# Two side buffers and 32 rows a step for ScalarE's pieces in both gather stages of a graph network kernel

## What is computed

```
h = relu(layernorm(x))
# layer 1: each edge fetches the row of its source node, transformed by its edge type
xW  = einsum('nd,rde->nre', h, W_rel)                 # 8 types
agg = segment_sum(xW[src, edge_type], dst)
y   = h + gelu(layernorm(agg + h @ W_self + b_conv) * g1 + b1n)
x   = x + y + gelu((layernorm(y) * g2 + b2n) @ W1 + b1) @ W2 + b2
# layer 2: attention over the same edges, 4 heads
h   = relu(layernorm(x));  xt = h @ W.T + bias
alpha = leaky_relu(alpha_src[src] + alpha_dst[dst])   # softmax over the edges of a target node
out = x + segment_sum(xt[src] * softmax(alpha), dst)
```

## Time and profile before

| quantity | value |
|---|---|
| median of three runs | 4349.86 us |
| time of the profiled execution | 4343.06 us |
| its span in the trace | 4341.3 us |
| POOL busy | 3081.9 us (71%) |
| DVE busy | 2539.8 us (59%) |
| PE busy | 2488.5 us (57%) |
| ACT busy | 860.6 us (20%) |
| mean granted TensorE clock | 0.745 of full speed |

### The profile page before, as it was taken

The page is one execution under the profiler, slowest core; times in us unless marked ns, Lnnn a source line. Parts: engine busy times, 40 slices in busy tenths (PEclk is TensorE's granted clock), DMA queues, the critical chain, the costliest instruction groups (busy, mean ns, idle before and its releaser), DMA issues.

```text
span 4341.3 us, 72570 instructions
## 1 busy us (share of the span) xinstructions
PE 2488.5 (57%) x13901; PEld 2078.1 (48%) x13902; DVE 2539.8 (59%) x7085; ACT 860.6 (20%) x2948; POOL 3081.9 (71%) x3262
## 2 busy tenths in 40 slices
PE   8833444444444444444455676766677667667675
PEld 3333344433433434343344565655566556556564
DVE  7742334444434443444445777777777777777776
ACT  5400111101110111110112222222222222222222
POOL 2177777777777777777737777777777777777774
PEclk9956767767767677677666877778877787787777
DMA  9622222222222222222214222222222222222221
GB/s 322 258 54 55 62 63 59 65 60 62 63 60 64 60 62 63 60 65 61 61 41 115 56 59 62 59 59 62 60 62 60 59 62 60 62 60 60 62 59 44
DMA packets 192089, 314.95 MB, mean 73 GB/s; under 512 B 69617, under 2 KB 123233, under 8 KB 190948
## 3 DMA queue, kind: packets, MB, share of 16 engines
q0 software_dynamic: 103424, 215.33, 21.4%
q1 hardware_dynamic: 38907, 68.15, 4.6%
q10 hardware_dynamic: 49310, 26.90, 2.2%
HBM read 238.52 MB, written 71.59 MB: 71 GB/s over the span
## 4 chain that ended last, share of the span: by engine, by line
POOL 37%; issue 25%; PE 22%; DVE 9%; ACTq 3%; ACT 2%; DMA 1%; DVEq 0%; POOLq 0%; SPq 0%
POOL G L646 37%; PE bank L1773 9%; PE quad L1818 3%; ACTq L819 2%; PE quad L1824 2%; PE quad L1813 1%; DVE A L1302 1%; PE quad L1860 1%; DMA xt_table<-w_all 1%; PE quad L1715 1%; PE bank L1715 1%; PE bank L1716 1%; PE quad L1716 1%; ACT w_all L894 1%; DVE stats L198 1%
## 5 line engine op out<-in xcount | busy, mean ns | idle before, releaser
L646 POOL DMA_INDIRECT G<-rel_table,idx x1600 | 1517.8, 949 | 633.9 <-issue 487.5
L646 POOL DMA_INDIRECT G<-xt_table,idx x1616 | 1526.8, 945 | 545.1 <-issue 545.1
L1906 PEld LDWEIGHTS quad<-ident,top 128*128 128x128 f32 x3328 | 569.4, 269 | 199.1 <-issue 198.2
L1906 PE MATMUL quad<-ident,top 128*128 128x128 f32 x3328 | 582.1, 356 | 119.9 <-DVEq L1507 119.7
L1267 DVE SCALAR_TENSOR_TENSOR agg<-bank,sel,agg 128x128 f32 x208 | 63.7, 347 | 821.1 <-PE bank L1773 809.0
L1937 PE MATMUL bank<-M,onehot 128*128 128x132 f32 x3328 | 445.4, 290 | 167.5 <-DVE M L1556 163.1
L1937 PEld LDWEIGHTS bank<-M,onehot 128*128 128x128 f32 x3328 | 411.2, 199 | 199.3 <-issue 199.3
L1773 PE MATMUL bank<-G,M 128*128 128x128 f32 x1616 | 267.3, 343 | 292.4 <-issue 278.6
L1773 PEld LDWEIGHTS bank<-G,M 128*128 128x128 f32 x1616 | 263.5, 259 | 296.7 <-issue 296.7
L1922 PE MATMUL bank<-Z,w_all 128*128 128x8 f32 x832 | 160.2, 321 | 378.4 <-DVEq L1524 253.5
L957 ACT ACTIVATE M<-G,M 128x32 f32<-128x32 f32 x1664 | 363.9, 308 | 13.3
(11 more groups left out here) (324 smaller groups left out, 3521.3 us busy)
## 6 DMA issues: line engine op xcount, KB each, us to landing
side<-rel_table SPq DMA_DIRECT2D x4736, 0.5 KB
side<-xt_table SPq DMA_DIRECT2D x4736, 0.5 KB
rel_table<-G SPq DMA_DIRECT2D x98, 512.0 KB, 3.4
G<-rel_table,idx POOLq DMA_INDIRECT x1616, 2.6
G<-xt_table,idx POOLq DMA_INDIRECT x1616, 7.1
side<-rel_table ACTq DMA_DIRECT2D x1408, 0.5 KB
side<-xt_table ACTq DMA_DIRECT2D x1408, 0.5 KB
xt_table<-w_all ACTq DMA_DIRECT2D x23, 264.0 KB
```

Source lines behind the costliest of these rows:

```text
L646: g.indirect_dma_start(out=G[:, s, c, 0:width], out_offset=None, in_=table, in_offset=bass.IndirectOffsetOnAxis(ap=idx[:, s, c:c + 1], axi ...
L1906: ins = t.matmul(banks[j][:, hd * P:(hd + 1) * P], top[:, j, hd:hd + 1].to_broadcast([P, P]), ident[:, :], start=False, stop=(hd == HEADS ...
```

## The change

ScalarE takes one piece in each of two groups in eight, in both stages: targets 16, 20, 24, ..., 96 (21 in place of 11). They alternate between two side buffers (`side` grows from 4 to 5 pieces, `x_res` shrinks to make room), so a target waits for the one two before it. In the first stage nothing else changes: 32 rows a step, in steps t-2 to t+1. In the attention stage a target takes four steps of 32 rows, t-6 to t-3, in place of eight steps of 16, t-10 to t-3. A step of 32 is two rounds of a load of 16 places and 16 DMAs (`ACT_ROWS = 16`).

```diff
-ACT_STEP = 8
+ACT_STEP = (4, 4)
+ACT_SIDES = 2
+ACT_LEAD, ACT_EACH = (2, 6), (32, 32)
...
-def by_act(g):
-    return ACT_FIRST <= g <= ACT_LAST and g % ACT_STEP == 0
+def by_act(k, g):
+    return ACT_FIRST <= g <= ACT_LAST and g % ACT_STEP[k] == 0
...
-        x_res = sb("x_res", [P, BLOCKS + SPARE, D])
+        x_res = sb("x_res", [P, BLOCKS + 2, D])
...
-        side = sb("side", [P, SIDES + 1, XT])
+        side = sb("side", [P, SIDES + ACT_SIDES, XT])
...
             def act_rows(k, gr, lo, hi):
-                q = ACTED.index(gr)
+                q = ACTED[k].index(gr)
+                b = q % ACT_SIDES
                 if lo == 0:
-                    act.wait_ge(act_line, 16 * (k * len(ACTED) + q + 1))
-                    if k == 0 and q:
-                        act.wait_ge(agg_done, ACTED[q - 1] + 1)
-                    elif k and q:
-                        act.wait_ge(side_moved, MOVED.index(ACTED[q - 1]) + 1)
+                    act.wait_ge(act_line, 16 * (k * len(ACTED[0]) + q + 1))
+                    if k == 0 and q >= ACT_SIDES:
+                        act.wait_ge(agg_done, ACTED[0][q - ACT_SIDES] + 1)
+                    elif k and q >= ACT_SIDES:
+                        act.wait_ge(side_moved, MOVED.index(ACTED[1][q - ACT_SIDES]) + 1)
                     elif k:
-                        act.wait_ge(agg_done, ACTED[-1] + 1)
+                        act.wait_ge(agg_done, ACTED[0][-1] + 1)
                     act_stop(act)
                 for p in range(lo, hi, ACT_ROWS):
                     places = load_places(mybir.EngineType.Activation, k, line[0:1, 2, p:p + ACT_ROWS], ACT_ROWS)
                     for j in range(ACT_ROWS):
-                        act.dma_start(row_into(k, SIDES, p + j), row_at(k, places[j])).then_inc(acted[k], 16)
+                        act.dma_start(row_into(k, SIDES + b, p + j), row_at(k, places[j])).then_inc(acted[k][b], 16)
-            def first_rows(gr):
-                for target in ACTED:
-                    if gr == target - 3:
-                        act_line_load(0, target)
-                    if 0 <= gr - (target - 2) < 4:
-                        act_rows(0, target, (gr - target + 2) * 32, (gr - target + 3) * 32)
-            def att_rows(gr):
-                for target in ACTED:
-                    if gr == target - 11:
-                        act_line_load(1, target)
-                    if 0 <= gr - (target - 10) < 8:
-                        act_rows(1, target, (gr - target + 10) * 16, (gr - target + 11) * 16)
+            def beside_rows(k, gr):
+                each = ACT_EACH[k]
+                for target in ACTED[k]:
+                    n = gr - (target - ACT_LEAD[k])
+                    if 0 <= n < P // each:
+                        act_rows(k, target, n * each, (n + 1) * each)
+                    if n == -1:
+                        act_line_load(k, target)
...
-                    att_rows(gr)
+                    beside_rows(1, gr)
```

More of the change, by code:

```diff
@@ L87, in by_sync, with by_rows, pieces, fetched @@
     return g <= ROW_LAST and g % ROW_OF in ROW_AT
-def by_act(g):
-    return ACT_FIRST <= g <= ACT_LAST and g % ACT_STEP == 0
-def by_rows(g):
-    return by_sync(g) or by_act(g)
+def by_act(k, g):
+    return ACT_FIRST <= g <= ACT_LAST and g % ACT_STEP[k] == 0
+def by_rows(k, g):
+    return by_sync(g) or by_act(k, g)
 ROWED = [g for g in range(GROUPS) if by_sync(g)]
[L100 to L105, removed]
+ACTED = [[g for g in range(GROUPS) if by_act(k, g)] for k in range(2)]
+MOVED = [g for g in range(GROUPS) if by_rows(1, g)]
+def pieces(k, g):
+    return CHUNKS - 1 if by_rows(k, g) else CHUNKS
 def seat2(g):
     return g % SLOTS
-def fetched(place, g):
-    return sum(16 * pieces(k) for k in range(g + 1) if place(k) == place(g))
+def fetched(k, g):
+    place = (seat, seat2)[k]
+    return sum(16 * pieces(k, b) for b in range(g + 1) if place(b) == place(g))
 def side_of(m):
@@ L405, in build @@
         rowed = [[sem(f"rowed{k}_{i}") for i in range(SIDES)] for k in range(2)]
-        acted = [sem("acted0"), sem("acted1")]
+        acted = [[sem(f"acted{k}_{i}") for i in range(ACT_SIDES)] for k in range(2)]
         act_line = sem("act_line")
@@ L464, in rows_there @@
         def rows_there(k, gr):
-            if by_act(gr):
-                return SIDES, (acted[k], 16 * P * (ACTED.index(gr) + 1))
+            if by_act(k, gr):
+                q = ACTED[k].index(gr)
+                return SIDES + q % ACT_SIDES, (acted[k][q % ACT_SIDES], 16 * P * (q // ACT_SIDES + 1))
             b, there = side_of(ROWED.index(gr))
@@ L655, in first_gather @@
                 pool_stop(pool)
-                gather(rel_table, seat(gr), D, gathered[0][seat(gr)], pieces(gr))
+                gather(rel_table, seat(gr), D, gathered[0][seat(gr)], pieces(0, gr))
             for gr in range(SLOTS):
@@ L695, in att_gather @@
                 pool_stop(pool)
-                gather(xt_table, s, XT, gathered[1][s], pieces(gr))
+                gather(xt_table, s, XT, gathered[1][s], pieces(1, gr))
             for s in range(SLOTS):
@@ L844, in load_indices @@
             def load_indices(gr):
-                act.wait_ge(gathered[0][seat(gr)], fetched(seat, gr) - 16 * pieces(gr))
+                act.wait_ge(gathered[0][seat(gr)], fetched(0, gr) - 16 * pieces(0, gr))
                 a.copy(idx[:, seat(gr), :], idx_all[:, gr, :]).then_inc(idx_ready[0], 1)
@@ L902, in quad_scalar @@
                     load_indices(n * SLOTS + FRONT + SLOTS)
-                    first_rows(n * SLOTS + FRONT + SLOTS)
+                    beside_rows(0, n * SLOTS + FRONT + SLOTS)
                 if own:
@@ L912, in quad_scalar @@
                     load_indices(n * SLOTS + FRONT + SLOTS + 1)
-                    first_rows(n * SLOTS + FRONT + SLOTS + 1)
+                    beside_rows(0, n * SLOTS + FRONT + SLOTS + 1)
                 first_gelu(n)
@@ L916, in quad_scalar @@
                     load_indices(n * SLOTS + FRONT + SLOTS + 2)
-                    first_rows(n * SLOTS + FRONT + SLOTS + 2)
+                    beside_rows(0, n * SLOTS + FRONT + SLOTS + 2)
                 forward(n)
@@ L920, in quad_scalar @@
                     load_indices(n * SLOTS + FRONT + SLOTS + 3)
-                    first_rows(n * SLOTS + FRONT + SLOTS + 3)
+                    beside_rows(0, n * SLOTS + FRONT + SLOTS + 3)
                 if own and not last:
@@ L982, in move_side @@
             def move_side(gr):
-                if gr < MAIN and by_rows(gr):
+                if gr < MAIN and by_rows(1, gr):
                     b, there = rows_there(1, gr)
@@ L995, in _ @@
             move_side(2)
-            next_indices(1, 0, 0, fetched(seat2, 0))
+            next_indices(1, 0, 0, fetched(1, 0))
             for i in range(0, (MAIN - 3) // SLOTS):
@@ L1001, in _ @@
                     move_side(gr + 2)
-                    next_indices(1, gr, (s + 1) % SLOTS, fetched(seat2, gr))
-                    att_rows(gr)
+                    next_indices(1, gr, (s + 1) % SLOTS, fetched(1, gr))
+                    beside_rows(1, gr)
                     if s == 1 and i >= LAG:
@@ L1626, in landed_in @@
             def landed_in(gr):
-                there = [(gathered[1][gr % SLOTS], fetched(seat2, gr))]
-                return there + [(side_moved, MOVED.index(gr) + 1)] if by_rows(gr) else there
+                there = [(gathered[1][gr % SLOTS], fetched(1, gr))]
+                return there + [(side_moved, MOVED.index(gr) + 1)] if by_rows(1, gr) else there
             scores(groups, c, 0, 0, landed_in(0))
@@ L1785, in add_group @@
             def add_group(g):
-                landed = [(gathered[0][seat(g)], fetched(seat, g))]
+                landed = [(gathered[0][seat(g)], fetched(0, g))]
                 if g == MAIN - 1:
                     landed = [(last_gathered[k], 16 * CHUNKS // PARTS) for k in range(PARTS)]
-                add_edges(g, seat(g), g % 2, landed, beside=g if by_rows(g) else None)
+                add_edges(g, seat(g), g % 2, landed, beside=g if by_rows(0, g) else None)
             for g in range(2):
```

## The result

The changed kernel takes 4501.77 us (median of 4 runs, 4500.29 to 4504.12) against 4349.52 us for the kernel before (4 runs, 4347.3 to 4353.6). The ratio is 1.0349, with a 95% interval of 1.0337 to 1.0361: slower by 3.5%. Its profiled execution has a span of 4502.1 us, against 4341.3 us.

The account below looks back on a forecast made before the run. POOL's gathers bound both stages; ACT's ring was to bound 84 attention rounds. 4343.06 + 165.3 (84 rounds) - 13.9 (last nine) - 12.5 (first stage) = 4482.0 us, given as 4485 us, range 4435 to 4545.

Parts of the forecast that it names:

- The 3 us added on top: Whole kernel: 4485 us given between 4482 and 4489, as the median of runs was 6.8 us above the profiled execution.
- The bound and the ring: Attention rounds 10 to 93: ACT's rows hold `hit` in an ACT, PE, DVE ring, making ACT the bound, +165.3 us.
- The two signs named ahead: Attention stage: PE's L1922 released by ACT's `hit` in nearly all 84 rounds; POOL at about 360 gathers in 500 us.
- The size of the ring: Attention rounds with rows: L951 to `hit` 15.65 us plus 5.70 us back to L951, 21.35 us a round.
- The 12.37 us for a step of 32: Median for 32 rows in the first stage, applied to attention; second sixteen cost 12.37 - 5.45 = 6.9 us.
- The last nine rounds: Attention rounds after 93, without rows: DVE at its own pace, seven rounds in 123 us instead of 137, -13.9 us.
- The first stage: First gather stage: POOL stays the bound and loses ten gathers of 1.25 us, -12.5 us.
- The other cover: First-stage dense block: PE's 7.11 us wait at the third group absorbs self products delayed some 14 us.
- Rows hidden in ACT's idle time: Rival, attention stage: second sixteen rows fit ACT's idle time, POOL bounds both stages, 4318 us; chance 0.05.
- The cheaper ring: Rival, attention stage: second sixteen rows cost 5.4 us, ring 19.85 us, about 4360 us; chance 0.07.
- the 8.75 taken for sixteen: Attention rounds: L951 to L943 with sixteen rows taken as 8.75 us, before 6.9 us for the second sixteen.
- The first stage lost nothing: Rival, first stage: four filled steps overrun dense blocks, 3 us for each of 21, about 4558 us; chance 0.10.

Follow-up runs that it names:

- the kernel with hit first: Changed kernel with attention rows issued behind the next round's `hit` copy: 4326.14 us, 0.9947 of the kernel before; on another chip 4318.67 us, 0.9950.
- The split kernel: Changed kernel with 16 of each attention step's 32 rows ahead of `hit` and 16 behind: 4319.98 us, 0.9951 of the kernel before.
- the kernel with one load: Changed kernel with one load of 32 places per step instead of two of 16: 4449.44 us, 1.0236 of the kernel before.

## Why the prediction was right

The forecast of 4485 us was 17 us below the measured 4501.77, and the time lies in the range. A little of that closeness is luck. The sum of 4482.0 us was made for a profiled execution, and that of the changed kernel took 4504.12 us, 22 us more. The 3 us added on top stood for runs that take longer than the profiled one, as in the kernel before; those of the changed kernel took less.

**The bound and the ring: right.** The reading of the earlier trace rows that ACT's rows hold `hit`, and of the earlier trace rows that `hit` closes a ring of 5.70 us, held in 84 rounds of 84; that the order in ACT's stream is the cause is shown by the kernel with hit first, which has the same rows and none of the loss. The two signs named ahead came: PE released by ACT's `hit` in 84 rounds, and POOL at 358 gathers in 500 us (about 360 forecast).

**The size of the ring: a little low.** Forecast 15.65 + 5.70 = 21.35 us, measured 15.79 + 5.74 = 21.53 us. The mis-sized terms are small ones: L949 to `hit` 0.14 us, the rest of the ring 0.04. Over 84 rounds they make the 15.6 us between +165.3 and +180.9, the largest part of the 22. The 12.37 us for a step of 32, read in the first stage, carried over: it is the median of the 84 steps of the attention stage too.

**The last nine rounds: right in kind, -10.5 in place of -13.9.** DVE ran at its own pace, but that is slower than the prediction took it: the seven rounds took 126.5 us and not 123. Four in a row take 17.7, 17.5, 18.7 and, with `finish`, 19.5 us. The 17.45 us of the earlier trace rows is the shortest kind, and I had counted all but the rounds with `finish` as 17.3.

**The first stage: right in direction.** All four kinds of step filled fit beside each other; rows of the fourth kind still end 2.8 us before ACT's second copy of the turned block, in the timeline of ACT of the changed kernel:

```profile
1069.60 12.42 ACTq L823 DMA_DIRECT2D side<-rel_table  x32
...
1084.85 0.60 ACT L878 ACTIVATE Y<-quad 128x512 f32<-128x512 f32 x1 [15.85 <-PE quad L1811]
```

The other cover was less sure than the prediction said: it calls the 7.11 us before PE's third group a wait for the gather, but the row says "issue", so it doesn't show what PE waited for.

The gain was 9.5 us in the trace and not 12.5. The two profiles differ in more than the change: the median gather takes 947 ns in the one of the changed kernel and 944 ns in the one before, and 3 ns over 1590 gathers are some 4 us. The split kernel and the second profile of the one with hit first have the same first stage and gathers of 944 ns; there L951 of round 10 starts at 2528.8 and 2526.7 us, 11.4 and 13.5 us before the 2540.2 of the earlier trace rows. So the 12.5 us are borne out.

**The rivals.** Rows hidden in ACT's idle time (4318 us) failed for the place, not for the amount: with the rows behind `hit`, they are hidden, and the gain is near the 25 us worked out for that rival (24, and 22 on another chip). The cheaper ring was refuted: with 32 rows ahead L949 to `hit` is 15.79 us, 7 more than the 8.75 taken for sixteen, and not 5.4. The first stage lost nothing.

**What issuing costs.** The Trainium skill says in "DMA: Bandwidth & Descriptors", section "Issuing engines are not separate DMA queues", that initiating a DMA is "usually small relative to the DMA itself". The prediction was right not to take the rows as free, but its words that this trace disagrees go too far for a single row. The last landing of a step came some 3 us after its last row was issued (by the semaphore updates in the trace of the changed kernel), while a step without a load in its middle holds ACT's stream for 10.74 us, or 0.34 us a row. What counts here is that the issues of 32 rows stand one behind another: in the round shown, 29 of them with a load of places held the stream for 10.89 us. What the same section says of several issuing engines, that they only save the sequencer's time, agrees with the kernel with hit first: it gained 24 us, where twenty gathers of 1.25 us left POOL.

## What to carry to other kernels

Issuing a DMA isn't counted as busy, but it holds the instruction stream of its engine: 32 row DMAs with the load of addresses in their middle took 12 to 13 us. Before such work is given to an idle-looking engine, find the ring of waits that passes through it, read its length from the one round in which this engine was the last, and put the work behind the step that others wait for. Here, against the kernel before, the same instructions made +152 us ahead of one copy and -24 us behind it.

## What the runs showed of the hardware

- The load of places (TENSOR_LOAD) on ACT took 1.19 us for 16 values and 2.14 us for 32. The second load of a step, right behind sixteen row DMAs, took 1.31 us on average in the changed kernel. So one load of 32 saves only 0.24 to 0.36 us against two of 16.
- A gather on POOL isn't of quite constant length. Its median is the same in both stages of one profile, and differs between profiles: 944, 945 or 947 ns. The line of the gathers of the first stage, of the changed kernel and of the second profile with hit first, which have the same first stage:

```profile
L650 POOL DMA_INDIRECT G<-rel_table,idx x1590: 941/947/2323, 203.1 to 2199.4; - x199
...
L650 POOL DMA_INDIRECT G<-rel_table,idx x1590: 940/944/2323, 203.1 to 2197.0; - x199
```

  The mean from start to start goes with it: in the first stage 1.254 us before and 1.256 after ((2199.4 - 203.1) / 1589), and in the attention stage of the kernel with hit first 1.2545 us ((4286.9 - 2273.4) / 1605), and 1.2520 in its second profile. The number of row DMAs beside the gathers isn't the cause: the kernel with one load, the split one and the second profile with hit first have all the rows of the changed kernel in both stages, and gathers of 944 ns. What differs between the executions stays open.
